# Output products behind the value projections, late gate and up halves beside the inverse, and a program without a loop

## The reference, cut to what matters

```
xn = (x - mean) / sqrt(var + 1e-5)
q, k, v = xn @ Wq, xn @ Wk, silu(xn @ Wv)          # 16 heads of 32
q, k = q / |q| * 32**-0.5, k / |k|;  beta = sigmoid(xn @ Wb)
for each token t and head:                          # recurrent delta rule
    delta = (v_t - k_t S) * beta_t;  S += outer(k_t, delta);  o_t = q_t S
attention = (rmsnorm(o) * o_norm_weight) @ Wo
ffn = ((silu(xn @ fp8(gate_w) * gs)) * (xn @ fp8(up_w) * us)) @ fp8(down_w) * ds   # 512 -> 1536 -> 512
```

## Time and profile before

| | |
|---|---|
| time, median of 3 runs | 2500.76 us (2495.1 to 2503.91) |
| the profiled execution: own time | 2507.98 us |
| its span | 2506.2 us |
| TensorE matmul busy | 2286.7 us, 91% |
| VectorE busy | 1836.6 us, 73% |
| ScalarE busy | 851.8 us, 34% |
| POOL busy | 267.2 us, 11% |
| mean granted TensorE clock | 0.995 |

### The profile page before, as it was taken

The page is one execution under the profiler, slowest core; times in us unless marked ns, Lnnn a source line. Parts: engine busy times, 40 slices in busy tenths (PEclk is TensorE's granted clock), DMA queues, the critical chain, the costliest instruction groups (busy, mean ns, idle before and its releaser), DMA issues.

```text
span 2506.2 us, 92909 instructions
## 1 busy us (share of the span) xinstructions
PE 2286.7 (91%) x40624; PEld 1267.3 (51%) x40944; DVE 1836.6 (73%) x3210; ACT 851.8 (34%) x2069; POOL 267.2 (11%) x521
## 2 busy tenths in 40 slices
PE   0588999999999998999989999999989999899996
PEld 0345555554555545455554555555454554555553
DVE  6895876869677685867759586686857768586775
ACT  2253332524234252432415233252422425233241
POOL 2001102010010201001010110201001010100100
PEclk9999999999999999999999999999999999999998
DMA  5100000000000000000000000000000000000000
GB/s 189 52 18 4 18 20 2 22 16 18 20 19 19 3 19 20 18 20 19 19 4 18 20 19 20 3 27 12 18 21 19 19 3 19 20 19 20 17 22 19
DMA packets 27203, 54.67 MB, mean 22 GB/s; under 512 B 5152, under 2 KB 5152, under 8 KB 26784
## 3 DMA queue, kind: packets, MB, share of 16 engines
q1 hardware_dynamic: 26784, 48.55, 5.5%
HBM read 31.76 MB, written 16.78 MB: 19 GB/s over the span
## 4 chain that ended last, share of the span: by engine, by line
PE 88%; DVE 6%; issue 5%; POOL 0%; ACT 0%; DMA 0%; SPq 0%; DVEq 0%; ACTq 0%; POOLq 0%
PE T L357 22%; PE D L438 21%; PE D L448 13%; PE D L449 13%; PE D L507 12%; PE D L373 7%; PE D L362 1%; DVE kpv L1239 1%; DVE outer_v L1141 1%; DVE kq L272 0%; DVE wgu L278 0%; DVE at L1148 0%; DVE at L852 0%; DVE outer_v L1234 0%; DVE fuse L1134 0%
## 5 line engine op out<-in xcount | busy, mean ns | idle before, releaser
L448 PE MATMUL D<-xt_hi,wgu 128*128 128x512 f16 x1536 | 582.3, 379 | 5.3 <-DVE kpv L1015 3.9
L449 PE MATMUL D<-xt_lo,wgu 128*128 128x512 f16 x1536 | 582.1, 379 | 0.0
L438 PE MATMUL D<-xt_hi,w_hi 128*128 128x512 f16 x832 | 318.7, 383 | 7.5 <-issue 7.5
L438 PE MATMUL D<-xt_lo,w_hi 128*128 128x512 f16 x832 | 318.0, 382 | 0.0
L438 PE MATMUL D<-xt_hi,w_lo 128*128 128x512 f16 x768 | 293.8, 383 | 0.0
L1148 DVE TENSOR_TENSOR at<-at,outer_v 128x62 f32<-128x62 f32 (+15 forms) x496 | 263.3, 531 | 15.5
L507 PE MATMUL D<-wd,f_lo 128*128 128x512 bf16 x640 | 242.6, 379 | 30.7 <-issue 30.7
L1141 DVE TENSOR_TENSOR outer_v<-mt,at 128x62 f32<-128x62 f32 (+15 forms) x496 | 260.0, 524 | 9.4
L448 PEld LDWEIGHTS D<-xt_hi,wgu 128*128 128x128 f16 x1536 | 150.3, 98 | 192.1 <-DVE fuse L1134 8.7
L449 PEld LDWEIGHTS D<-xt_lo,wgu 128*128 128x128 f16 x1536 | 150.3, 98 | 178.6
L507 PE MATMUL D<-wd,f_hi 128*128 128x512 bf16 x576 | 218.3, 379 | 20.3 <-issue 20.3
(11 more groups left out here) (163 smaller groups left out, 3163.5 us busy)
## 6 DMA issues: line engine op xcount, KB each, us to landing
xs<-_attn_hidden_states_dram SPq DMA_DIRECT2D x34, 512.0 KB, 3.6
out_dram<-xs SPq DMA_DIRECT2D x32, 512.0 KB, 2.9
kq<-in_L_ffn_gate_w_dram SPq DMA_DIRECT2D x3, 768.0 KB, 4.4
kq<-in_L_ffn_up_w_dram SPq DMA_DIRECT2D x3, 768.0 KB, 4.4
f_hi<-in_L_ffn_down_w_dram SPq DMA_DIRECT2D x2, 768.0 KB, 5.7
f_lo<-in_L_ffn_down_w_dram SPq DMA_DIRECT2D x2, 768.0 KB, 7.2
qt<-in_L_attn_Wq_dram SPq DMA_DIRECT2D x1, 1024.0 KB, 8.6
kpv<-in_L_attn_Wk_dram SPq DMA_DIRECT2D x1, 1024.0 KB, 10.9
```

What stands on the lines that cost most here:

```text
L438: last = nc.tensor.matmul(D[bank][:, :], w[:, k, cols], xp[:, k, :], start=n == 0, stop=n == len(products) - 1)
L448: nc.tensor.matmul(D[bank][:, :], wgu[:, k, c:c + P], xt_hi[:, k, :], start=k == 0, stop=False)
L449: last = nc.tensor.matmul(D[bank][:, :], wgu[:, k, c:c + P], xt_lo[:, k, :], start=False, stop=k == KT_ - 1)
```

## The change

The output products of the span before all stand behind the value projections (48 in place of 24). Of the 24 halves of gate and up, 20 follow them, and the last four are cut in two and put behind the eight groups with the inverse. The fillings of the chain are six down products each, and the next span's transpositions come a step earlier. VectorE, ScalarE and POOL get orders to match: all four output additions lie in the solve, fused gates start at operation 29, nine of them in the solve and three behind; half of the value scalings come ahead of the first silu; statistics of the next x lie between the reads of the products with the inverse. In the preparation VectorE rounds two pieces while the maxima are reduced, and the projections of the first span start as soon as their own weights are ready; the other four pieces, the norms (now in bank D0, behind the value projections) and the bounds are worked during the first span. POOL's two pieces wait for the normalised x. All 16 spans are written out.

```diff
-TURNS = 4
-JOB_..., JOB_WO, JOB_GU, JOB_DN = ..., (13, 14, 39, 40), 15, 41
-XT_AT = {2: 0, 3: 1, 5: 2, 6: 3}
+TURNS = SPANS
+JOB_..., JOB_WO, JOB_GU, JOB_DN = ..., (13, 14, 15, 16), 17, 41
+XT_AT = {1: 0, 2: 1, 4: 2, 5: 3}
-OUT_AT = {16: 0, 18: 1}
-FUSE_AT = {20: 0, 24: 1, 28: 2, 32: 3, 36: 4, 40: 5, 44: 6, 49: 7, 54: 8, 59: 9}
-VK_AT = {ic: range(6 * ic - 6, min(6 * ic, 64)) for ic in range(1, 12)}
-STATS_AT, AGGREGATE_AT, APPLY_AT = {2: 1}, {0: 0, 3: 1}, {1: 0, 4: 1}
-Q_SUM_AT, Q_SUM_FIRST = {0: 0}, {3: 1, 5: 2, 6: 3}
-DOWN_AT = {1: 0, 4: 1, 6: 2, 7: 3}
-FILL_FIRST, FILL_UW, FILL_CHAIN = 8, 4, 5
+OUT_AT = {16: 0, 20: 1, 23: 2, 25: 3}
+SCALE_AT = 8
+FUSE_AT = {29: 0, 33: 1, 36: 2, 39: 3, 42: 4, 46: 5, 49: 6, 54: 7, 59: 8}
+LOW_BEFORE, LATE_HALVES = 8, 4
+VK_FIRST = 32
+VK_AT = {ic: range(VK_FIRST + 4 * ic, VK_FIRST + 4 * ic + 4) for ic in range(8)}
+APPLY_AT, APPLY_LATE = {2: 1}, {0: 0}
+Q_SUM_AT, Q_SUM_FIRST = {3: 0}, {4: 1, 6: 2, 7: 3}
+DOWN_FIRST, DOWN_AT = {3: 0, 5: 1}, {6: 2, 7: 3}
+FILL_CHAIN = 6
...
 # SyncE: pieces 0 and 1 first, pieces 4 to 7 into qt and pt
+            sp.wait_ge(proj_ready, 2)
+            load_piece(P_PIECES + 2)
+            sp.wait_ge(proj_ready, 5)
+            load_piece(P_PIECES + 3)
...
 # TensorE
             pe.wait_ge(proj_ready, 5)
-            pe.wait_ge(ffn_ready, 1)
-            pe.wait_ge(v_rounded, GU_PIECES - P_PIECES)
...
+                        if opening and JOB_GU <= job < JOB_GU + 4 and bank_of(job) == NORM_BANK:
+                            pe.wait_ge(bound2_ready, 1)
...
-                    if not opening:
+                    if opening:
+                        pe.wait_ge(v_raw, MS)
+                        for n in range(GU_PIECES):
+                            pe.wait_ge(sq_ready, n + 1)
+                            # 12 products with ones into D[NORM_BANK]
+                    else:
                         pe.wait_ge(olo_ready, since(1))
-                        for j in range(2):
+                        for j in range(TILES):
                             project_out(j, take(JOB_WO[j]))
-                    for half in range(2 * IC):
+                    for half in range(2 * IC - LATE_HALVES):
                         gate_up(half)
...
-                        fill(FILL_FIRST + g * FILL_UW, FILL_UW)
+                        gate_up(2 * IC - LATE_HALVES + g // 2, 2 * (g % 2), 2 * (g % 2) + 2)
...
 # ScalarE
+                    for n in range(VK_FIRST):
+                        values_by_k(n)
...
                     for g in range(8):
+                        if g in (2, 6):
+                            silu_gate(early + g // 4)
                         copy_u(g)
+                        if g == 4:
+                            high_part(early)
+                    high_part(IC - 1)
...
 # POOL
+            pool.wait_ge(xn_ready, TILES)
+            pool.wait_ge(unit_ready, P_PIECES)
...
+                    if opening:                    # behind k_norm_ready
+                        pool.wait_ge(bound2_ready, 1)
+                        pool.nop(nofuse=True)
+                        nc.gpsimd.tensor_tensor(b_b[:, :], b_a[:, :], pos_half[:, :], ALU.pow).then_inc(bound_ready, 1)
...
 # VectorE
+            for n in range(P_PIECES, P_PIECES + 2):
+                rounded(n, v_rounded)
             dve.wait_ge(amax_summed, 1)
...
+                    def prepare_first():
+                        for n in range(P_PIECES + 2, GU_PIECES):
+                            rounded(n, v_rounded)
+                            if n == P_PIECES + 3:
+                                b_to_tokens()
...
+                        read_grams(0)
+                        mask_products(0)
+                        for m in range(MS):
+                            k_to_tokens(m)
+                        beta_to_problems()
+                        beta_over_k(0)
+                        times_beta(0)
+                        for n in range(2):
+                            rounded(GU_PIECES + n, wd_rounded)
+                            dve.wait_ge(wd_rounded, n + 1)
+                        for m in range(MS):
+                            v_to_tokens(m)
+                        for n in range(2, 4):
+                            rounded(GU_PIECES + n, wd_rounded)
+                            dve.wait_ge(wd_rounded, n + 1)
+                        gate_up_bound()
+                        set_diagonal(0)
...
-            some_spans(0, first=True)
-            with dve.Fori(1, SPANS // TURNS) as it:
-                some_spans(it)
+            all_spans()
```

More of the change, by code:

```diff
@@ L66, in bank_of @@
     return job % 4 if job < JOB_DN + 3 else JOB_DN % 4
-FILL_FIRST, FILL_UW, FILL_CHAIN = 8, 4, 5
[L70 to L77, removed]
+FILL_CHAIN = 6
 def fill_at(c, half):
-    return FILL_FIRST + 8 * FILL_UW + (2 * c + half) * FILL_CHAIN
+    return (2 * c + half) * FILL_CHAIN
 def dense_order():
-    order = [("job", n) for n in range(JOB_WO[2])]
-    first = 0
+    order = [("job", n) for n in range(JOB_DN)]
     for c in range(STEPS):
[L90 to L98, removed]
+        if c in XT_AT:
+            order.append(("xt", XT_AT[c]))
+        if c % 2:
+            order.append(("job", JOB_DN + c // 2))
     return {name: n for n, name in enumerate(order)}
@@ L385, in _, with all_spans @@
                 transpose_xn(j, b)
[L387 to L392, removed]
             pe.wait_ge(proj_ready, 5)
-            pe.wait_ge(ffn_ready, 1)
-            pe.wait_ge(v_rounded, GU_PIECES - P_PIECES)
-            def some_spans(it, first=False):
+            def all_spans(it=0):
                 for turn in range(TURNS):
                     par = turn % 2
-                    opening = first and turn == 0
+                    opening = turn == 0
                     def since(per_span, n=0):
@@ L440, in project, with gate_up @@
                         if n == len(products) - 1:
-                            last.then_inc(dense_done, 3 if opening and job == JOB_V[MS - 1] else 1)
-                    def gate_up(half):
-                        bank = take(gate_up_job(half))
+                            last.then_inc(dense_done, 1 + TILES if opening and job == JOB_V[MS - 1] else 1)
+                    def gate_up(half, first=0, end=KT_):
+                        bank = bank_of(gate_up_job(half)) if first else take(gate_up_job(half))
                         ic, side = divmod(half, 2)
                         c = side * INNER + ic * P
-                        for k in range(KT_):
+                        for k in range(first, end):
                             nc.tensor.matmul(D[bank][:, :], wgu[:, k, c:c + P], xt_hi[:, k, :], start=k == 0, stop=False)
@@ L450, in gate_up @@
                                                     start=False, stop=k == KT_ - 1)
-                        last.then_inc(dense_done, 3 if opening and half == 2 * IC - 1 else 1)
+                        if end == KT_:
+                            last.then_inc(dense_done, 1)
                     def gram(g):
@@ L510, in down, with fill @@
                             last.then_inc(dense_done, 1)
[L512 to L524, removed]
+                    def fill(first):
+                        down(first // 24, first % 24, first % 24 + FILL_CHAIN)
+                    if opening:
+                        pe.wait_ge(ffn_ready, 1)
                     pe.wait_ge(kt_ready, since(MS, MS))
@@ L1115, in some_spans @@
+                    (prepare_first if opening else prepare)()
                     read_grams(1)
@@ L1196, in some_spans @@
                     for op in range(2 * (CHUNK - 1)):
-                        if op in V_AT:
+                        if op in V_AT and not opening:
                             v_to_tokens(V_AT[op])
+                        if opening and op == SCALE_AT:
+                            gate_up_scale()
                         if op == P_AT:
```

207 lines of the change are left out of this document (97 added, 110 removed).

## The result

The changed kernel takes 2443.7 us (median of 4 runs, 2442.0 to 2446.3) against 2501.5 of the kernel before (4 runs, 2495.1 to 2503.91): a ratio of 0.9774 (0.9753 to 0.9795), 57.8 us or 2.3% less.

The account below looks back on a forecast made before the run. TensorE was taken to bound the kernel, with products nearly all the time. Loop -12.3, usual spans -3.5 and opening -5.3 give -21.1 us, forecast 2480 on the runs' median of 2500.76; range 2458 to 2499.

Parts of the forecast that it names:

- The loop: Writing out all 16 spans removes two jumps back, with idle and slow products: 12.3 us gained, or 0.
- The usual spans: Spans after the opening: +16.5 for the inverse, -5.7 for the subtraction, -14.3 for issue gaps, together -3.5 us.
- The wait for the inverse: TensorE reaches the products with the inverse too early: 1.1 us a span, 16.5 us lost, bounds 9 and 20.
- the feeding of the gates: VectorE's fused gates come in time for TensorE's gate and up products, with 1.4 to 2.4 us left.
- the late halves: Gate/up products between the groups with the inverse: cost 0, at most 10 us in 15 spans.
- the end of the wait for the subtraction: TensorE's wait for VectorE's subtraction at the chain's last step goes: 5.7 us gained, bounds 2 and 6.
- every one of the 66 gaps shrinks by one product: Sixth product per chain filling shortens TensorE's issue gaps, 34.2 us in all: 14.3 us gained, bounds 0 and 22.
- The opening: First span: earlier projections, inverse 7.8 us earlier, chain 8.8 us earlier less 3.5 us of fillings: gain 5.3, bounds 0 and 12.
- the wait for the root: In the first solve VectorE waits 3.7 us for POOL's square root of the bounds, now behind the key norms.
- That the inverse is in time: Rival: VectorE's short waits close more than counted, so the 16.5 us are not lost: 2463 us, chance 0.22.
- That the fillings bring nothing: Rival: neither the chain's sixth products nor the opening gain anything: 2499.6 us, chance 0.17.
- that the solve bounds the span: Rival: late fused gates hold the solve up, TensorE waits 3 us a span before the inverse: 2508 us, chance 0.11.

Follow-up runs that it names:

- a body that runs once: Kernel before with the first block and the loop body eight spans each, so no jump back is taken inside: 2477.85 us, ratio 0.9927.
- the doubled product: First down product of each of the chain's 16 fillings issued twice: 2513.19 us on the kernel before, 2492.32 us on the changed one.
- the second profile of the kernel before: The kernel before, unchanged, run once more for its profile: 2501.05 us.
- six jumps: Kernel before with two spans written out and a body of two spans run seven times: 2511.92 us, ratio 1.0037.

## Why the prediction was right in direction and wrong in size

**The loop**, predicted 12.3. Measured 22.5 on the kernel before, 18 on the changed one, 18.7 by a body that runs once. The step that failed is "Nothing else changes in how instructions come". The idles and the slow products were sized rightly (12.3 and 13.2 in two profiles, and the granted clock is at 1.2 GHz for 6.8 and 3.4 us there), but with a body of four spans three chains have a further wait of about 1.8 us and are longer by some 8 us together. The remainder, 2 us or so, is within what profiles of one kernel differ by; what the register operations cost, perhaps 0.2 us a span in the changed order, is untested in the order of before.

**The usual spans**, predicted -3.5. Against the kernel before written out they are 146.75 - 145.02 = 1.73 us shorter, 26 in 15 spans. The wait for the inverse was right: 0.93 a span against 1.1, and removing it gave back 12.8 against 16.5 on the books. So were the feeding of the gates (no gate product waits in usual spans), the late halves at no cost (the inverse stage is 16.79 after 16.73) and the end of the wait for the subtraction. The term that was mis-sized is "every one of the 66 gaps shrinks by one product", 14.3 us, with the 5.7 beside it: 20.0 in all. Measured against the kernel before, the chain takes in 3.45 us of products and gets 0.22 shorter, 3.67 x 15 = 55 us; 1.13 x 15 = 17 of these come with the loop's removal, 38 with the order. So the order gave 38 where 20 were on the books. Two errors lie in it. I took the 34.2 us of listed gaps for the whole loss, when a chain bound by products would be 4.2 us shorter, 63 us in 15 spans: a break of under 0.15 us, and the time around a longer one, is in no listed gap. Inside the chain's groups of small products alone the kernel before takes 54 us more than the changed one with the doubled product, where the listed gaps differ by 31 (written out 36 and 18, after 7 and 3). And I took a filling to shrink each gap by itself, when the stretch from the inverse to the end of the chain lasts about what its instructions need, 57 to 58 us for some 3,330 of them (24 x 128 small ones, 2 for each of 112 long products, 32 for transpositions; before, 58.0; two products behind the inverse and six in the chain, 58.3; written out, 56.9; after, with 32 more, 57.84): products put into it are nearly free until they bind it, wherever they come from. The 63 us rest on the extrapolated 37.05; the 38 and the 55 do not.

The Trainium skill, page "Runtime: NRT & Kernel Launch", section "Instruction fetch mechanics", says that instructions come in blocks of 256 and that crossing a block is mostly hidden. The trace agrees with the first (gaps at one place of 256, 256.1 records a packet) and disagrees with the second for these small products: by what the Trainium skill says the doubled product would cost about 55 us on either kernel, an estimate; it cost 11.5 on the one before. The Trainium skill, same page and section, also says that a taken branch stalls the engine when its target has to be fetched first. The trace agrees: each jump here shows 3.0 to 4.1 us of idle.

**The opening**, predicted 5.3. The terms held: projections at 58.25 (59.3 said), the solve from 122.8 (124.6), the wait for the root 4.30 (3.7), the chain's first product at 193.66 (194.3; 203.13 before). The timelines:

```profile
122.78 0.22 DVE L1145 TENSOR_TENSOR outer_v<-mt,at 128x62 f32<-128x62 f32 x1
```

```profile
193.66 1.32 PE L350 MATMUL T<-kq,state 32*32 32x64 f32 x64 [0.22 <-ACT kpv L679]
```

The first span ends 10.4 us earlier, or 7.7 against the second profile of the kernel before, whose second span starts at 242.53. The 3.5 us that I charged for the chain's 16 more long products were not paid: the chain there is 41.1 us against 42.1 (39.0 in the second profile), the same error as above.

**The rivals.** That the inverse is in time was wrong (0.93 us), though its time, 2463, came nearer, by luck. That the fillings bring nothing was wrong; that the solve bounds the span too. The sum of what was measured closes: 22.5 for the loop, 26 for the spans and 10.4 (or 7.7) for the opening are 59 (56) against 57.8. All three terms came out larger than forecast, by 10, 22.5 and 5 (or 2) us.

## What to carry to other kernels

Where small matmuls follow each other, count TensorE's instructions between two unexplained gaps; if the count is constant, the stretch is short of instructions, and long products moved into it are free until they bind it. Size such a loss against a variant with one product more in each place, which shows the bound by products, and not by the gaps that the profile lists. A loop can cost more than the idle and the slow products at its jump: here it did with a body of four and not with a body of two, so measure it written out. Look at the instruction counts of a variant before reading its time: the loop that ran once had lost the operations it was to test.

## What was not expected of the hardware

A jump back costs 3.0 to 4.1 us of idle and 0.2 to 3.1 us of slower products behind it, at six jumps as at two. TensorE's instructions came in blocks of 256 about every 4.8 us in the chain of the kernel before, and it stood still for up to 1.8 us at a block's end, inside a group that waits for nothing. Long products beside short ones can be nearly free: 256 more of them, 55 us of work, cost 11.5. What stays open is why a body of four spans meets its three waits of 1.8 us, what the register operations cost in the order of before, and what sets the time between two blocks.
